# A Trainium2 megakernel, last stage: sixth projection beside the feed-forward products, four rotary buffers, low half of tokens from PSUM

## The reference, cut to what matters

```python
def shift_tokens(t):
    a, s = jnp.split(t, 2, -1)
    s = jnp.pad(s, ((0, 0), (1, 0), (0, 0)))[:, :-1]
    return jnp.concatenate([a, s], -1)

def attn_layer(x, Wqkv, qs, ksc, Wo):
    q, k, v = jnp.split(x @ Wqkv, 3, -1)
    q, k, v = (sh(q), sh(k), sh(v))        # 16 heads of 64
    q, k = l2norm(q) * qs, l2norm(k) * ksc
    q = q * cos * scale + rotate_half(q) * sin * scale
    k = k * cos * inv + rotate_half(k) * sin * inv
    out = local_attention(q, k, v)         # windows of 32, softmax(8 q k')
    return out.transpose(0, 2, 1, 3).reshape(b, n, INNER) @ Wo

def ffn_layer(x, g, bln, W1, b1, W2, b2):
    xn = (x - mu) / jnp.sqrt(var + 1e-05) * g + bln
    a, gate = jnp.split(xn @ W1 + b1, 2, -1)
    return a * jax.nn.gelu(gate, approximate=False) @ W2 + b2

for i in range(DEPTH):                     # 6
    x = attn_layer(shift_tokens(x), Wqkv[i], q_scale[i], k_scale[i], Wo[i]) + x
    x = ffn_layer(shift_tokens(x), ln_g[i], ln_b[i], W1[i], b1[i], W2[i], b2[i]) + x
```

## Time and profile before

| | us |
|---|---|
| runs | 4209.45, 4209.49, 4212.79 (median 4209.49) |
| profiled execution, own time | 4207.12 |
| its span, first to last instruction | 4205.3 |
| busy PE, DVE | 3880.3 (92%), 3528.0 (84%) |
| busy ACT, POOL | 2636.6 (63%), 2381.6 (57%) |

### The profile page before, as it was taken

How to read it: one execution, slowest core, us unless ns; L and a number is a source line. 1 busy time by engine, 2 the same in 40 slices (tenths; PEclk the granted TensorE clock), 3 DMA queues, 4 the chain that set the end, 5 groups by cost and what they waited for, 6 DMA issues and landing times.

```text
span 4205.3 us, 120168 instructions
## 1 busy us (share of the span) xinstructions
PE 3880.3 (92%) x48128; PEld 2725.0 (65%) x48128; DVE 3528.0 (84%) x5537; ACT 2636.6 (63%) x5550; POOL 2381.6 (57%) x2045
## 2 busy tenths in 40 slices
PE   3457998999995999999999999999999999999998
PEld 1225776777774676767776676666766676666765
DVE  6875556777776999999999999999999999999997
ACT  3543336666664666676667666676667666666665
POOL 0111001000002887888878788888878787888885
PEclk7768999999997999999999999999999999999999
DMA  3000000000001333233333333233332333233332
GB/s 105 0 0 1 1 1 1 1 0 0 0 0 41 75 92 82 62 84 89 78 75 70 80 90 82 62 84 91 77 78 67 80 90 82 65 81 75 84 85 65
DMA packets 264675, 238.95 MB, mean 57 GB/s; under 512 B 31716, under 2 KB 260328, under 8 KB 263400
## 3 DMA queue, kind: packets, MB, share of 16 engines
q1 hardware_dynamic: 264168, 231.82, 23.6%
HBM read 26.20 MB, written 4.19 MB: 7 GB/s over the span
## 4 chain that ended last, share of the span: by engine, by line
PE 71%; DVE 13%; ACT 7%; issue 4%; POOL 2%; SPq 2%; DMA 1%; DVEq 0%; ACTq 0%; POOLq 0%
PE bank L1990 13%; PE bank L1923 13%; PE bank L2008 8%; PE bank L1963 7%; PE bank L2050 5%; PE bank L854 4%; ACT arena L1129 3%; PE bank L1956 2%; PE bank L2063 2%; DVE arena L1016 2%; PE bank L1934 2%; DVE arena L1026 2%; PE bank L1254 1%; PE bank L1245 1%; SPq L2169 1%
## 5 line engine op out<-in xcount | busy, mean ns | idle before, releaser
L1451 DVE TENSOR_TENSOR arena<-bank,tab 128x1024 f32<-128x1024 f32 x768 | 935.4, 1218 | 179.7 <-ACT arena L1683 108.0
L1846 POOL TENSOR_TENSOR arena<-arena 128x512 f32<-128x512 f32 x768 | 1011.8, 1333 | 52.1 <-DMA arena<-arena 47.9
L1683 ACT ACTIVATE arena<-bank 128x512 f32<-128x512 f32 x768 | 458.2, 597 | 518.7 <-PE bank L1923 510.0
L1923 PE MATMUL bank<-x_split,wqk_split 128*128 128x256 f32 x4608 | 717.8, 299 | 41.9 <-DVE arena L1451 27.5
L1990 PE MATMUL bank<-m_vo,arena 128*32 128x512 f32 x6144 | 753.9, 597 | 2.1 <-DVE arena L1544 1.1
L1923 PEld LDWEIGHTS bank<-x_split,wqk_split 128*128 128x128 f32 x4608 | 603.5, 191 | 185.5 <-issue 94.4
L1854 POOL TENSOR_TENSOR arena<-arena 128x256 f32<-128x256 f32 x768 | 559.0, 739 | 152.3 <-ACT arena L1683 151.9
L1707 ACT ACTIVATE arena<-bank 128x512 f32<-128x512 f32 x768 | 457.5, 596 | 182.0 <-PE bank L1990 178.9
L1863 POOL TENSOR_TENSOR arena<-arena 128x1024 f32<-128x1024 f32 x192 | 372.8, 1942 | 240.3 <-DVE arena L1499 240.3
L1187 POOL TENSOR_TENSOR x_all<-x_all,arena 128x256 f32<-128x256 f32 x16 | 11.6, 728 | 832.6 <-DVE arena L1008 832.6
L1869 POOL TENSOR_TENSOR arena<-arena 128x1024 f32<-128x1024 f32 x192 | 372.3, 1940 | 122.7 <-DVE arena L1512 122.7
(11 more groups left out here) (258 smaller groups left out, 7115.9 us busy)
## 6 DMA issues: line engine op xcount, KB each, us to landing
arena<-arena SPq DMA_DIRECT2D x1536, 128.0 KB, 2.5
wqk_stage<-in_wqk SPq DMA_DIRECT2D x6, 1024.0 KB, 8.5
out_x<-x_all SPq DMA_DIRECT2D x7, 512.0 KB, 5.0
wvt<-in_wvt SPq DMA_DIRECT2D x6, 512.0 KB, 4.6
wo<-in_wo SPq DMA_DIRECT2D x6, 512.0 KB, 5.7
arena<-in_wbh SPq DMA_DIRECT2D x1, 2048.0 KB, 9.6
w<-in_w SPq DMA_DIRECT2D x6, 341.0 KB, 5.7
wqk_stage<-out_x SPq DMA_DIRECT2D x8, 128.0 KB, 2.4
```

The source lines that it names most:

```text
L1451: nc.vector.tensor_tensor(d_t[c % KS].rearrange("p k h t -> p k (h t)"), bank[c % 2][:, :].unsqueeze(1).to_broadcast([P, 2, 2 * T]), tab[: ...
L1683: nc.scalar.activation(d_sq[i % 4].rearrange("p h t -> p (h t)"), bank[c % 2][:, :], ACT.Square).then_inc(s_sq, 1)
L1846: nc.gpsimd.tensor_tensor(d_rot[i // 4][:, i % 4, :, :], t[:, :, 0, :], t[:, :, 1, :], ALU.add).then_inc(s_ad, 1)
L1923: last = nc.tensor.matmul(bank[c % 2][:, h * T:(h + 1) * T], wqk_split[:, i, wp, h, :], x_split[:, n % 2, xp, :], start=(q == 0), stop=(q ...
```

## The change

PE does the projection chunk 5 right behind the two `ffn_up` and ahead of the first half of the scores. The rotary product of chunk 3 moves from the start of the next turn to the end of its own, with a fourth `d_t` buffer. The second rotary, the softmax sums, the gates and the norm's two steps change places on VectorE. The low half of the tokens is taken from bank 6, in two instructions of 64 partitions at the start of the turn; the attention, which overwrites bank 6, waits for it. On ACT `norm_high` and the first read of token products go ahead of `softmax_exp` (except in the turn with `head_matrices`). On POOL the weight splits are spread over the turn.

```diff
-        KS = 3
+        KS = 4
@@ split_low_tokens
-                nc.vector.tensor_tensor(x_split[:, n % 2, 1, :], d_xt[n % 3], x_split[:, n % 2, 0, :].bitcast(F32), ALU.subtract)\
-                    .then_inc(s_split, 1)
+                at_least(dve, s_proj, CHUNKS * (n - 1))
+                first, second, now = slice(0, C // 2), slice(C // 2, C), n % 2
+                nc.vector.tensor_tensor(x_split[first, now, 1, :], bank[6][first, 0:T],
+                                        x_split[first, now, 0, :].bitcast(F32), ALU.subtract)
+                nc.vector.tensor_tensor(x_split[second, now, 1, 1:], bank[6][second, 0:T - 1],
+                                        x_split[second, now, 0, 1:].bitcast(F32), ALU.subtract).then_inc(s_split, 1)
@@ phase_d_vector, the turn
+                split_low_tokens(f)
                 turn_probabilities(f - 3, 1)
-                rotary_products(f - 1, 3)
...
-                split_low_tokens(f)
-                ffn_gate(f - 4, 2)
                 norm_weight(f - 1)
+                norm_factor(f - 1)
                 residual(f - 3)
-                norm_factor(f - 1)
...
+                rotary_products(f, 2)
                 softmax_sum(f - 2, 0)
-                rotary_products(f, 2)
...
-                softmax_sum(f - 2, 1)
-                softmax_reciprocal(f - 2, 1)
+                rotary_products(f, 3)
...
                 ffn_residual(f - 4)
+                softmax_sum(f - 2, 1)
+                softmax_reciprocal(f - 2, 1)
@@ phase_d_gpsimd, the turn
+                if fresh:
+                    split_low(pool, layer_of(f), 2, 3)
                 scale_shifted(f - 2, 1)
+                add_halves(f, 0, 1)
                 if fresh:
-                    split_low(pool, layer_of(f), 4, 5, 6, 7)
-                add_halves(f, 0, 1, 2, 3)
+                    split_low(pool, layer_of(f), 4, 5)
+                add_halves(f, 2, 3)
...
@@ phase_d_tensor, attention and the turn
+                    pe.wait_ge(s_split, min(n + 4, TOTAL))
...
+                project(f - 1, 5)
                 scores(f - 2, 0)
-                project(f - 1, 5)
```

More of the change, by code:

```diff
@@ L1355, in build @@
         STORES = ((0, 4), (4, 8), (8, 12), (12, 15), (15, 16))
-        ZEROS = 7
+        ZEROS = 8
         TURNS_D = TOTAL + 4
@@ L1592, in phase_d_vector @@
                 nc.vector.memset(v, 0.0).then_inc(s_zero, 1)
+            nc.vector.memset(x_split[:, :, 1, 0:1].bitcast(F32), 0.0).then_inc(s_zero, 1)
             dve.wait_ge(s_stats, 8)
@@ L1605, in phase_d_vector @@
             for f in range(TURNS_D):
+                split_low_tokens(f)
                 turn_probabilities(f - 3, 1)
-                rotary_products(f - 1, 3)
+                rotary_products(f - 1, 4)
                 ffn_gate(f - 4, 0)
-                rotary_products(f - 1, 4)
+                rotary_products(f - 1, 5)
                 softmax_maximum(f - 2, 0)
-                rotary_products(f - 1, 5)
                 softmax_shift(f - 2, 0)
@@ L1614, in phase_d_vector @@
                 ffn_gate(f - 4, 1)
+                ffn_gate(f - 4, 2)
                 softmax_maximum(f - 2, 1)
-                split_low_tokens(f)
-                ffn_gate(f - 4, 2)
                 norm_weight(f - 1)
+                norm_factor(f - 1)
                 residual(f - 3)
-                norm_factor(f - 1)
                 rotary_products(f, 0)
@@ L1789, in phase_d_scalar @@
                 next_fresh = here(f + 1) and (f + 1) % SEQS == 0
+                turned = here(f - 2) and (f - 2) % SEQS == 0
                 read_products(f - 3, 7)
@@ L1809, in phase_d_scalar @@
                 norm_rsqrt(f - 1)
-                if here(f - 2) and (f - 2) % SEQS == 0:
+                if turned:
                     head_matrices(layer_of(f - 2))
-                softmax_exp(f - 2, 0)
-                squares(f, 0)
                 norm_high(f - 1)
-                read_products(f - 2, 0, 1, 2)
+                if turned:
+                    softmax_exp(f - 2, 0)
+                    squares(f, 0)
+                    read_products(f - 2, 0)
+                else:
+                    read_products(f - 2, 0)
+                    softmax_exp(f - 2, 0)
+                    squares(f, 0)
+                read_products(f - 2, 1)
                 squares(f, 1)
+                read_products(f - 2, 2)
                 if fresh and f:
@@ L1885, in phase_d_gpsimd @@
                 rotary_sums(f - 1, 6, 7)
+                if fresh:
+                    split_low(pool, layer_of(f), 2, 3)
                 scale_shifted(f - 2, 1)
+                add_halves(f, 0, 1)
                 if fresh:
-                    split_low(pool, layer_of(f), 4, 5, 6, 7)
-                add_halves(f, 0, 1, 2, 3)
+                    split_low(pool, layer_of(f), 4, 5)
+                add_halves(f, 2, 3)
+                if fresh:
+                    split_low(pool, layer_of(f), 6)
                 softmax_scale(f - 2, 0)
+                if fresh:
+                    split_low(pool, layer_of(f), 7)
+                if next_fresh:
+                    split_low(pool, layer_of(f + 1), 0, 1)
                 softmax_scale(f - 2, 1)
-                if next_fresh:
-                    split_low(pool, layer_of(f + 1), 0, 1, 2, 3)
         def phase_d_tensor(pe):
```

## The result

| | us |
|---|---|
| before, 6 runs beside it | median 4211.26 (4209.45 to 4217.12) |
| after, 6 runs | median 4430.57 (4405.95 to 4959.36) |
| ratio | 1.0506, 95% interval 1.0482 to 1.0529 |
| profiled execution of after, its span | 4441.9, 4440.1 |

The run of 4959 us had a lower granted clock (0.739) and is left out of the ratio; the other five have a median of 4419.24. The forecast was 4239. The direction was right, the size was not: +208 us by that median where +29 was expected.

What follows compares the result with a forecast made beforehand. PE sets the old pace; in the new order a loop through all engines, 29.68 us a turn, was to bound the kernel. Ordinary turns +42, layers -12, jitter -3, pipe ends +2: +29, to 4239 us, range 4208 to 4258.

Steps and rivals of the forecast that it cites:

- The bound and the loop: Loop through POOL, DVE, ACT and PE sets the new turn: sum 29.71 us, taken as 29.68, bounds 29.55 to 29.9.
- PE waits at `norm_split`: PE waits each turn at `spread_norms` 0 for DVE, 0.75 us, and at `sum_squares` 1 for POOL, 0.3.
- The bound for PE's own work: PE's turn if nothing else gave way: 29.20 less 0.3 and 0.26, 28.64 us.
- The loop's first line: POOL from rotary sum 0 to the end of `scale_shifted`, called ten instructions: 12.13 us.
- The low half: DVE's `split_low_tokens`, 1.36 us, becomes two PSUM halves of about 0.4 each, some 0.7, giving 0.6 back.
- Projection 4 and first turns: PE's wait before projection 4 goes, 0.26 us; first turns of layers, 31.25 us, become 30.0.
- `norm_factor` waits for the end of `scale_shifted`: On DVE, `norm_factor` waits 0.6 us for POOL, ends 0.34 later and wakes ACT 0.03 later: 0.37 us in the loop.
- Rival 3: The lock bites twice or `norm_factor` meets a rotary sum: +0.4 us a turn on top, 4275 us; chance 0.08.
- PE's saving of 0.3 by the transition: On PE, one narrow stretch fewer in the new order of scores and projection: 0.2 to 0.35 us a turn, taken 0.3.
- The sum without the passing over: Whole kernel: ordinary turns +42, layers -12, jitter -3, pipe ends +2, together +29, 4239 us; no passing over included.

Runs made afterwards that it cites:

- e12: Kernel after, with GpSimd's `add_halves` 4 also waiting for rotary product 4, a pause of 0.30 us: 4278.2 us, ratio 1.0164 to the kernel before.
- e10: Kernel after, with GpSimd's rotary sums 4 and 5 cut into four and three pieces, no pause: 4674.63 us, ratio 1.1112 to the kernel before.
- e3: Kernel after, with `norm_weight`'s result in PSUM and ACT's order of before: 4188.34 us, ratio 0.9948 to the kernel before.
- e5: e1 with the low half taken from SBUF in one instruction again, at the new place: 4227.99 us, ratio 1.0038 to the kernel before.
- e1: Kernel after, with `norm_weight` writing to bank 7, so `norm_factor` has one PSUM operand: 4212.76 us, ratio 1.0005 to the kernel before.
- m5: m4 with both operands in SBUF and 0 to 17 more GpSimd sums ahead, stretches 12.2 to 23.7 us: from 14.9 us all 336 passed over.
- e6: e1 with `scores` back ahead of projection 5 on PE: 4223.27 us, ratio 1.0026 to the kernel before.
- e8: Kernel after, with GpSimd waiting for ACT's last norm step ahead of `scale_shifted`: 4338.3 us, ratio 1.0299 to the kernel before.
- m1: Separate kernel, four GpSimd instructions back to back against one VectorE instruction: two SBUF operands 0.41 to 1.98 us, one in PSUM 0.411 to 0.416.
- e9: Kernel after, with `add_halves` 7 also waiting for rotary product 5, which had ended before, so no pause: 4438.05 us, ratio 1.0542 to the kernel before.
- e2: Kernel after, with ACT's order of before and `norm_factor` keeping two SBUF operands: 4242.16 us, ratio 1.0073 to the kernel before.
- e4: Kernel after, with the residual between `norm_weight` and `norm_factor`: 4436.55 us, ratio 1.0506 to the kernel before.
- e11: Kernel after, with `add_halves` 4 waiting for a rotary product that had ended before, so no pause: 4400.23 us, ratio 1.0432 to the kernel before.
- m3: m2 with a pause behind GpSimd's seventh instruction: all let in at the next change but 6 of 420.
- m2: m1 with ten GpSimd instructions ahead of the scale and two sums behind: all let in at the next change but 16 of 420.
- m4: m2 with VectorE issuing the pair of norm steps: with both operands in SBUF, all let in at the next change but 18 of 295.

## Why the prediction was wrong, by its steps

- **The bound and the loop: right in length.** 29.71, taken as 29.68, and turns of 29.67 to 29.68 us where nothing is passed over. PE waits at `norm_split` as named, for less (0.35 us in the short turn shown, 0.75 named), and not at `sum_squares` for GpSimd; that wait stands in the lists of e12 (the second row below) and e10 alone. The other wait of a short turn, 0.22 us ahead of the scores for VectorE, was not named. The bound for PE's own work was wrong: 28.64 us were taken, and PE is busy for 29.09 in the short turn and 28.80 in e3. Since the loop set the turn, this did not show in the time. The loop's first line says ten GpSimd instructions and rightly adds up eleven. The rows, the short turn first and then e12:

```profile
2592.41 0.50 PE L1965 MATMUL bank<-z_split,sel_r 128*128 128x256 f32 x2 [0.35 <-DVE z_split L1476]
```

```profile
PE bank L1956 <- POOL arena L1867: 21.1, 88, 0.3
```
- **The low half: right.** 0.38 and 0.43 us, starts 0.39 apart, so the second begins only when the first has ended; the 0.6 us saved stand in e5 against e1 as 15 us.

```profile
2575.32 0.38 DVE L1441 TENSOR_TENSOR x_split<-bank,x_split 64x256 fp32r<-64x256 f32 x1
2575.71 0.43 DVE L1443 TENSOR_TENSOR x_split<-bank,x_split 64x255 fp32r<-64x255 f32 x1
```

- **Projection 4 and first turns: right.** Before projections 0.9 us of waits are left of 11.6, and in e1 some first turns take 29.95 us (30.0 was taken); those with `head_matrices` take 31.3.
- **"`norm_factor` waits for the end of `scale_shifted`", 0.37 in the loop: the step that failed.** 42 of 96 are short (31 ordinary turns of 29.6 to 29.8 us). In the other 54 the wait goes on to the end of GpSimd's stretch, +2.5 us (3.38 against 0.88). e12, e10 and m5 show what makes it so: GpSimd has by then run about 14 us or more without a pause. Nothing in the trace of before could show it, because its stretches at such meetings were 5.3 and 3.9 us. But the lengthening stood in my own loop: GpSimd going straight from `softmax_scale` (1.86) to the end of `scale_shifted` (12.13) is 14.0 us, the length at which both outcomes occur. What the prediction lacked is any price for being passed over at a change.
- **Rival 3 had the place and the sign, not the price.** "The lock bites twice, +0.4 a turn" was worth 0.08; a second and third refusal cost 2.5 us in 54 turns.
- **The clock was no term at all.** In the short turn shown, with 0.6 us of idle PE, the granted clock stayed at 1.00; with 2.6 us in two waits close together it fell in most turns and cost 1.6 us each time; a fall is counted in 36 turns.
- **PE's saving of 0.3 by the transition: too high.** e6 finds 10 us, about 0.1 a turn, though other bounds lie near. It did not set the time.
- **The sum without the passing over was near.** e8 less its 1.0 us and e12 less its 0.35 us a turn, over 88 turns, give 4249 and 4247, against 4239.

The Trainium skill, SBUF — State Buffer, section SBUF: two separate sides, says that the loser is blocked for the whole instruction of the other engine. m1 agrees (408 of 408). m5 goes beyond it: after a long stretch the loser is blocked through the instruction that it met and all that follow without a pause, 3 in m5 and in the loop of the kernel, 5 in first turns of layers.

**What stays open.** Why 14 us, and whether it is time, as m5 and the kernel suggest (12 instructions of GpSimd in the kernel, 15 in m5 at the step), or work done; no run here varies the one without the other. Nor does the length sort all cases of the kernel. The second `norm_factor` of the stage was passed over at a stretch of 12.1 us in the kernel after and in e9, and of 12.8 us in e10, while in e2, e4 and e11 all six with 12.1 us were let in. A few short ones in e2, e4, e9 and e11 had 14.03 to 14.11 us, and of three in the kernel after that asked in a rotary sum behind the scale, with 14 to 15 us behind them, two were let in and one not. Which stall makes the clock fall was not tried.

## What to carry to other kernels

Look for every VectorE instruction with two SBUF operands that runs while GpSimd works, and measure how long GpSimd has had no pause when they meet; around 14 us and above deserves suspicion: an order that closes its small gaps can turn a wait for one instruction into a wait for all of them. Moving one operand to a free piece of PSUM removes the meeting at no cost (e1). Put such an instruction where nobody waits for it: the same lock-out cost 1.2 us a turn in e2 and 2.5 to 4.1 in the kernel after, because the change had put ACT's exponential and squares behind it.

## What the runs showed of the hardware that was not expected

- A pause of 0.30 us in GpSimd's work, 8 us ahead, takes `norm_factor` from 3.35 us in the median to 0.88.
- From a stretch of 14.9 us on, 336 of 336 askers were passed over; at 13.5 and less none of 72 (m5). The kernel has exceptions at 12.1 and 12.8 us.
- An instruction that asks shortly ahead of GpSimd's next change comes too late for it and is let in one change later, and the margin grew with the stretch: with 2.1 us behind GpSimd nobody came too late, though 8 asked 0.04 to 0.08 us ahead (m1); with 4.5 us those at 0.05 did and those at 0.09 did not (m3); with 10 to 12 us those up to 0.09 (m2) and 0.116 (m4) did, and those from 0.12 on did not.
- The loser also costs the winner: a rotary sum that follows a meeting takes 1.48 us, not 1.29, in the kernel after.
- Two short stalls of PE, 0.99 and 1.65 us, were followed by 4 us at a granted clock of 0.57. In 34 turns with such a pair the clock fell, in 13 it did not.
